# Gate and up projections with 480 moving columns: one pass of the high weights over high and low tokens

## The chip, the cores and the metric

The kernel runs on one core of one Trainium2 chip. The time is device time in microseconds (us) of the whole program, from several executions. A core has five engines with instruction streams of their own: TensorE (PE in the profile, with its weight loads as PEld), VectorE (DVE), ScalarE (ACT), GpSimd (POOL) and SyncE (SP), which issues most DMAs here. They meet through semaphores.

## The reference

One layer on x of 8 batches x 64 tokens x 1024:

```python
x = x + cross_attention(layernorm(x), context)   # 8 x 1601 context rows and the 64 new ones
x = x + self_attention(layernorm(x))             # 16 heads, rotary, causal
xn = layernorm(x)
weights = golden_weights(xn, Wr, temperature)    # which of 8 experts, with which weight
gate = jnp.einsum('btd,edf->betf', xn, Wg)
up = jnp.einsum('btd,edf->betf', xn, Wu)
h = jax.nn.silu(gate) * up
e_out = jnp.einsum('betf,efd->betd', h, Wd)
x = x + jnp.einsum('bte,betd->btd', weights, e_out)
```

All is float32. The cross attention uses one head of width 1024. Each expert has three 1024 x 1024 matrices.

## The kernel before, in words

**Two parts for a float32.** Every float32 operand of a product is split into a high part (rounded to fp32r) and a low part (the rest). A product is made of three matmuls: high x high, high x low, low x high (`three`, L1425 to L1428; which of its three lines carries which pair depends on the argument order). Weights and context stream in as *units* of 128 x 2048 float32 (1 MB). SP loads a unit into a ring slot `raw` (L426), ScalarE copies it to `hi` (L628), VectorE subtracts to get `lo` (L939), and then TensorE uses it. `hi` and `lo` have four slots (RING). ScalarE and VectorE split unit k + 3 (AHEAD) in the program's order before their own work for unit k.

**Experts.** For each expert the tokens that chose it, 240 at most (CAP), are gathered, turned (L1903) and split: `xg[:, c, 0:240]` holds the high parts of feature chunk c, `xg[:, c, 240:480]` the low parts, side by side. An expert has 12 units. Units 0 to 7 (f in the code) each hold 128 gate rows and 128 up rows (j = 0, 1), 8 chunks c each. So one unit is 2 x 8 x 3 = 48 matmuls of 240 columns into one PSUM bank `ps[:, f % 2, ...]`, gate in its first half and up in its second. Then ScalarE makes silu of the gate out of PSUM (L904), VectorE multiplies by up out of PSUM (L1390), rounds to `h_hi` (L1393) and subtracts to `h_lo` (L1395). `h_split` counts these. Units 8 to 11 are the down projection, 96 matmuls of 512 columns into banks `Y_BANK`; ScalarE scales them into y (L912), and GpSimd adds y to the output by an indirect DMA (L531).

**What binds the order.** TensorE may begin unit f (from 2 on) only when `h_split` says that unit f - 2, whose bank it takes over, is done. After unit 2 TensorE multiplies the next expert's token list (`list_item`, L1891), for which VectorE builds `sel` and `item_list` after its work for unit 1 (`build_list`, L1346, L1348). VectorE begins each expert with `take_target` (L1364, L1366), which waits until all scatters of the expert before have landed. ScalarE begins it with the split of unit 3, which waits for unit 0 (`gu_ready`). Units are written out in the program's text; experts 0 to 6 are a loop, and the last one follows it.

**Cross attention.** Batches b = 0 to 7 follow each other; while the values of batch b are used, the keys of b + 1 are multiplied. `ATTENTION` is the list of units, and each engine's `attention` goes through it. For the first batch, ScalarE takes the exponentials of the scores (`exps`, L692) in its step for the last key unit (u = 6); TensorE needs them for `turn_weights(0)` (L1551), which stands before unit 3 of the next batch's keys.

## Time and profile before

| | us |
|---|---|
| median of 3 runs | 1269.14 |
| the runs | 1261.70, 1269.14, 1269.29 |
| the profiled execution, its own time | 1264.38 |
| its span | 1262.6 |
| TensorE busy | 1200.4 (95%) |
| VectorE busy | 818.9 (65%) |
| ScalarE busy | 633.1 (50%) |

The profile is of one execution. Its time exceeds the span by 1.8 us. The cross attention ends near 425 us, the self attention and the router follow, and the experts run from 709 us to the end. Busy shares are over the whole span; a TensorE matmul counts as busy from its start to the modelled end of its pipeline, so matmuls overlap in these numbers, and the pace is read from start to start.

### The profile page before, as it was taken

The numbers are of one execution on the slowest core, as the hardware profiler recorded it, in microseconds if no ns is written. First come the engines' busy times: TensorE is split into PE (matmuls) and PEld (weight loads), VectorE is DVE, ScalarE is ACT, GpSimd is POOL, SyncE is SP. The second block draws the span as 40 slices with busy tenths as digits, with TensorE's granted clock in tenths as the row PEclk, the third lists the DMA queues.
The fourth block names the chain that finished last, engine by engine and source line by source line (L and its number), as shares of the span: only waits on it lengthen the run. The fifth ranks groups of instructions, "written<-read, shape, count | busy, mean of one in ns | idle before, by whom it ended". The sixth has DMA issues, their size and how long they took to land.

```text
span 1262.6 us, 19328 instructions
## 1 busy us (share of the span) xinstructions
PE 1200.4 (95%) x7810; PEld 1050.4 (83%) x7810; DVE 818.9 (65%) x1026; ACT 633.1 (50%) x604; POOL 95.7 (8%) x74
## 2 busy tenths in 40 slices
PE   5999999999998999999997699999999999999996
PEld 5888777777777878888886698989898999999895
DVE  7336789989999566463565674747565655656465
ACT  4124889888897423123543345344444444454431
POOL 0010000000000000000000012121111111121202
PEclk9999899999999999999999799999999999999998
DMA  7445899999998624220234376766667666676642
GB/s 290 146 159 192 308 352 360 376 373 363 379 383 333 248 77 171 96 100 34 101 143 167 113 251 166 262 197 226 202 216 212 200 227 200 217 210 230 172 160 33
DMA packets 46872, 272.98 MB, mean 216 GB/s; under 512 B 5880, under 2 KB 6024, under 8 KB 18528
## 3 DMA queue, kind: packets, MB, share of 16 engines
q1 hardware_dynamic: 36768, 243.48, 52.8%
q0 software_dynamic: 10048, 28.71, 9.4%
q8 instruction: 40, 0.66, 0.2%
q14 instruction: 16, 0.13, 0.0%
HBM read 255.92 MB, written 16.25 MB: 216 GB/s over the span
## 4 chain that ended last, share of the span: by engine, by line
PE 77%; DVE 8%; ACT 6%; issue 4%; DMA 4%; POOLq 0%; SPq 0%; POOL 0%; ACTq 0%; DVEq 0%
PE ps L1426 21%; PE ps L1427 21%; PE ps L1428 21%; PE ps L1539 6%; DVE lo L939 5%; ACT hi L628 4%; DMA out<-y,target 3%; PE ps L1652 2%; PE ps L1903 1%; PE ps L1587 1%; DVE stats L943 1%; ACT scores L692 1%; DMA raw<-weights 1%; PE ps L1745 1%; PE ps L1729 1%
## 5 line engine op out<-in xcount | busy, mean ns | idle before, releaser
L939 DVE TENSOR_TENSOR lo<-raw,hi 128x2048 fp32r<-128x2048 f32 (+1 forms) x198 | 443.4, 2251 | 160.3 <-ACT hi L628 157.9
L628 ACT ACTIVATE hi<-raw 128x2048 fp32r<-128x2048 f32 (+1 forms) x198 | 370.5, 1882 | 252.2 <-PE ps L1428 241.3
L1426 PE MATMUL ps<-act_hi,hi 128*128 128x240 f32 (+2 forms) x1232 | 360.7, 293 | 7.4 <-DVE act_lo L965 4.1
L1428 PE MATMUL ps<-act_hi,lo 128*128 128x240 f32 (+2 forms) x1232 | 361.6, 294 | 0.0
L1427 PE MATMUL ps<-act_hi,hi 128*128 128x240 f32 x1024 | 282.8, 276 | 0.0
L1426 PEld LDWEIGHTS ps<-act_hi,hi 128*128 128x128 f32 x1232 | 234.2, 190 | 16.7 <-issue 5.4
L1428 PEld LDWEIGHTS ps<-act_hi,lo 128*128 128x128 f32 x1232 | 234.6, 190 | 6.9
L1427 PEld LDWEIGHTS ps<-act_hi,hi 128*128 128x128 f32 x1024 | 193.5, 189 | 0.3
L1426 PE MATMUL ps<-hi,act_hi 128*128 128x512 f32 x320 | 126.4, 395 | 0.0
L1428 PE MATMUL ps<-hi,act_lo 128*128 128x512 f32 x320 | 124.9, 390 | 0.0
L1427 PE MATMUL ps<-lo,act_hi 128*128 128x512 f32 x320 | 124.8, 390 | 0.0
L904 ACT ACTIVATE xq<-ps 128x240 f32<-128x240 f32 x64 | 23.7, 370 | 164.4 <-PE ps L1428 164.3
L1539 PE MATMUL ps<-hi,qs 128*128 128x512 f32 (+1 forms) x256 | 94.6, 381 | 7.8 <-DVE lo L939 7.8
L1426 PE MATMUL ps<-hi,h_hi 128*128 128x512 f32 x256 | 101.3, 396 | 0.0
L1427 PE MATMUL ps<-lo,h_hi 128*128 128x512 f32 x256 | 101.0, 394 | 0.0
L1428 PE MATMUL ps<-hi,h_lo 128*128 128x512 f32 x256 | 101.0, 394 | 0.0
L1652 PE MATMUL ps<-hi,pt 128*128 128x512 f32 (+1 forms) x208 | 86.4, 415 | 6.4 <-DVE lo L939 5.1
L1539 PE MATMUL ps<-lo,qs 128*128 128x512 f32 (+1 forms) x256 | 91.5, 372 | 0.0
L1652 PE MATMUL ps<-lo,pt 128*128 128x512 f32 (+1 forms) x208 | 83.2, 400 | 0.0
L939 DVE TENSOR_TENSOR lo<-raw_more,hi 128x2048 fp32r<-128x2048 f32 (+2 forms) x38 | 76.8, 2032 | 8.3 <-ACT hi L628 8.3
L1427 PE MATMUL ps<-act_lo,hi 128*128 128x512 f32 (+1 forms) x208 | 78.4, 377 | 0.0
L531 POOL DMA_INDIRECT out<-y,target x32 | 51.8, 1617 | 307.3 <-ACT y L912 305.1
(228 smaller groups left out, 1431.2 us busy)
## 6 DMA issues: line engine op xcount, KB each, us to landing
raw<-weights SPq DMA_DIRECT2D x124, 1024.0 KB, 4.9
raw<-keys SPq DMA_DIRECT2D x36, 1024.0 KB, 5.8
raw<-context SPq DMA_DIRECT2D x31, 1024.0 KB, 8.3
raw_more<-context SPq DMA_DIRECT2D x17, 1024.0 KB
raw_more<-keys SPq DMA_DIRECT2D x12, 1024.0 KB
xq<-x_in SPq DMA_DIRECT2D x4, 512.0 KB, 6.8
raw_more<-weights SPq DMA_DIRECT2D x4, 512.0 KB
new_keys_t<-kvs POOLq DMA_DIRECT2D x8, 256.0 KB, 3.6
```

The lines of the kernel that those rows point to most:

```text
L531: pool.indirect_dma_start(out_d.rearrange("t (g d) -> (t g) d", g=2), bass.IndirectOffsetOnAxis(ap=target[0:R, g, n:n + 1], axis=0), y[0:R ...
L628: act.activation(part(hi, k, kind), part(raw, k, kind), ACT.Copy).then_inc(hi_done, 1)
L692: act.activation(S[rows, :], S[rows, :], ACT.Exp, bias=nb[rows, :], scale=SCALE, accum_out=sums[rows, :]).then_inc(p_ready, 1)
L904: act.activation(silu[:, k % 2, :], ps[:, k % 2, 0:CAP], ACT.Silu).then_inc(silu_done, 1)
L939: dve.tensor_tensor(part(lo, k, kind), part(raw, k, kind), part(hi, k, kind), ALU.subtract).then_inc(lo_done, 1)
L943: steps.done(dve.bn_stats(stats[:, t, h, :], x[:, t, h * HALF:(h + 1) * HALF]))
L1426: pe.matmul(out, a_hi, b_hi, start=first, stop=False)
L1427: pe.matmul(out, a_hi, b_lo, start=False, stop=False)
L1428: return pe.matmul(out, a_lo, b_hi, start=False, stop=last)
L1539: ins = pe.matmul(scores_at(j, slice(0, P)), qs[:, s % 2, cc, :], buf[:, k % RING, c * w:(c + 1) * w], start=(cc == 0 and b == 0), stop=(c ...
L1587: ins = pe.matmul(out, O[:, c * P:(c + 1) * P], twice[:, 0:QL], start=True, stop=(s < LATE))
L1652: ins = pe.matmul(ps[:, 6 + h, :], pt[rows, kc, :], buf[rows, k % RING, at], start=(kc == 0 and b == 0), stop=(kc == NCH - 2 and b == 1))
```

## The change

Three edits. First, the gate and up products: the matmul of the high weights now has 480 moving columns, high and low tokens in one pass, and a second matmul of the low weights adds 240 columns. Gate and up of a unit take a bank each (`GU_BANK`: banks 0 and 1, or 6 and 7), and bank columns 240 to 480 hold a partial sum that has to be added: ScalarE copies these out of PSUM for gate and up (480 columns in all), VectorE adds the first halves out of PSUM to the copy in SBUF (`gate_up`), ScalarE makes silu of the gate, and VectorE multiplies, both out of SBUF. The first down half uses banks 0 and 1 and waits for `h_split` of unit 6 (7) in its first unit and of unit 7 (8) in its second. TensorE waits at an expert's end until the first two y are copied. Second, `gate_up` lies over x, so ScalarE waits once for the copy of x to the output; bank 7 held the first list, so unit 0 waits for `first_listed`. Third, the exponentials of batch 0 move behind the split of one more unit.

```diff
--- before.py
+++ after.py
@@ -308,6 +308,9 @@
         rows_turned = sem("rows_turned")
         xg_hi = sem("xg_hi")
         xg_done = sem("xg_done")
+        first_listed = sem("first_listed")
+        gu_copied = sem("gu_copied")
+        gu_added = sem("gu_added")
         gu_ready = sem("gu_ready")
         h_split = sem("h_split")
         h_padded = sem("h_padded")
@@ -383,7 +386,7 @@
             earlier_expert = route_c[:, CAP + NE:CAP + NE + NE * NE]
             token_id, token_p, token_t = (route_c[:, CAP + NE + NE * NE + j * TT:CAP + NE + NE * NE + (j + 1) * TT]
                                           for j in range(3))
-        silu = xq[:, TT * D:TT * D + 2 * CAP].rearrange("p (s n) -> p s n", s=2)
+        gate_up = xq[:, 0:4 * CAP].rearrange("p (s j n) -> p s j n", s=2, j=2)
         spare = xq[:, TT * D:TT * D + 2 * TT * NE * NE].rearrange("p (s n) -> p s n", s=2)
         logits_t = xq[0:NE, TT * D:TT * D + TOK]
         xg = act_hi
@@ -552,7 +555,8 @@
         LIST_BANK = 5
         SUM_AT = (NCH - 8) * QL + 8
         FIRST_BANK = 7
-        Y_BANK = (6, 2)
+        Y_BANK = (0, 2)
+        GU_BANK = (0, 6)
         LN_BANK = 4
         LOGITS_BANK = 3
         LOGITS_T_BANK = 2
@@ -754,6 +758,8 @@
                         block_copy(ATTENTION[n - 1][2])
                     if what == "keys":
                         s = b - 1
+                        if u == 0 and s == 0:
+                            exps(0)
                         if u == 0 and copied < blocks_before(n):
                             new_v_copy(copied)
                             copied += 1
@@ -768,7 +774,6 @@
                             if b == 0:
                                 new_v_copy(copied)
                                 copied += 1
-                                exps(0)
                     elif what == "values":
                         s = b
                         if u == 0 and s == B - 1:
@@ -900,8 +905,14 @@
 
                         split(u0 + k + AHEAD, PER_EXPERT, e, used=(gu_ready, 8 * e + 1) if k == 0 else None)
                     if k < 8:
+                        bank = GU_BANK[k % 2]
                         act.wait_ge(gu_ready, 8 * e + (k + 1))
-                        act.activation(silu[:, k % 2, :], ps[:, k % 2, 0:CAP], ACT.Silu).then_inc(silu_done, 1)
+                        if k >= 2:
+                            act.wait_ge(h_split, 8 * e + (k - 1))
+                        act.activation(gate_up[:, k % 2, :, :], ps[:, bank:bank + 2, CAP:2 * CAP],
+                                       ACT.Copy).then_inc(gu_copied, 1)
+                        act.wait_ge(gu_added, 8 * e + (k + 1))
+                        act.activation(gate_up[:, k % 2, 0, :], gate_up[:, k % 2, 0, :], ACT.Silu).then_inc(silu_done, 1)
                     if k == 7 and more:
                         turned_hi(e + 1)
                     if k in (9, 11):
@@ -913,6 +924,7 @@
                                            scale=target_w[0:R, n:n + 1]).then_inc(y_done, 1)
 
             turned_hi(0)
+            act.wait_ge(scattered, 16)
             with act.Fori(0, NE - 1) as e:
                 item(e, U_FFN, False, True)
             item(NE - 1, U_FFN, False, False)
@@ -1292,8 +1304,9 @@
             dve.tensor_copy(item_list[:, :, :], token_w[:, :, 0:1, :].rearrange("p t a k -> p t (a k)"))\
                .then_inc(sel_built, 1)
             dve.wait_ge(list_summed, 1)
-            dep(dve.tensor_copy(listed[0:R, :, 2:LIST], ps[0:R, FIRST_BANK, 0:NT * 8].rearrange("p (n k) -> p n k", k=8)
-                                [:, :, 2:LIST]))
+            dve.tensor_copy(listed[0:R, :, 2:LIST], ps[0:R, FIRST_BANK, 0:NT * 8].rearrange("p (n k) -> p n k", k=8)
+                            [:, :, 2:LIST]).then_inc(first_listed, 1)
+            dve.wait_ge(first_listed, 1)
 
             def slot_values():
                 steps.done(dve.tensor_tensor(slot_token[0:R, :], listed[0:R, :, 0], listed[0:R, :, 1], ALU.add))
@@ -1386,13 +1399,16 @@
                     if more or k + AHEAD < PER_EXPERT:
                         split(u0 + k + AHEAD, PER_EXPERT, e)
                     if k < 8:
+                        bank, both = GU_BANK[k % 2], gate_up[:, k % 2, :, :]
+                        gate, up = both[:, 0, :], both[:, 1, :]
+                        dve.wait_ge(gu_copied, 8 * e + (k + 1))
+                        dve.tensor_tensor(both, ps[:, bank:bank + 2, 0:CAP], both, ALU.add).then_inc(gu_added, 1)
                         dve.wait_ge(silu_done, 8 * e + (k + 1))
-                        steps.done(dve.tensor_tensor(silu[:, k % 2, :], ps[:, k % 2, CAP:2 * CAP],
-                                                     silu[:, k % 2, :], ALU.mult))
+                        steps.done(dve.tensor_tensor(gate, up, gate, ALU.mult))
                         steps.wait()
-                        steps.done(dve.tensor_copy(h_hi[:, k, 0:CAP], silu[:, k % 2, :]))
+                        steps.done(dve.tensor_copy(h_hi[:, k, 0:CAP], gate))
                         steps.wait()
-                        dve.tensor_tensor(h_lo[:, k, 0:CAP], silu[:, k % 2, :], h_hi[:, k, 0:CAP],
+                        dve.tensor_tensor(h_lo[:, k, 0:CAP], gate, h_hi[:, k, 0:CAP],
                                           ALU.subtract).then_inc(h_split, 1)
                     if k == 1 and more:
                         build_list(e + 1, bass.ds(e + 1, 1))
@@ -1920,13 +1936,18 @@
                         pe.wait_ge(h_split, 8 * e + (f - 1))
                     elif f == 0:
                         pe.wait_ge(routed, 1)
+                        pe.wait_ge(first_listed, 1)
                     for j in range(2):
                         for c in range(C):
                             if f == 0 and j == 0 and c % 2 == 0:
                                 pe.wait_ge(xg_done, 4 * e + (c // 2 + 1))
                             at = slice(j * D + c * P, j * D + (c + 1) * P)
-                            ins = three(ps[:, f % 2, j * CAP:(j + 1) * CAP], hi[:, k % RING, at], lo[:, k % RING, at],
-                                        xg[:, c, 0:CAP], xg[:, c, CAP:2 * CAP], c == 0, c == C - 1)
+                            out = ps[:, GU_BANK[f % 2] + j, 0:2 * CAP]
+                            if c == C - 1:
+                                pe.matmul(out[:, 0:CAP], lo[:, k % RING, at], xg[:, c, 0:CAP], start=False, stop=False)
+                            ins = pe.matmul(out, hi[:, k % RING, at], xg[:, c, 0:2 * CAP], start=c == 0, stop=c == C - 1)
+                            if c < C - 1:
+                                pe.matmul(out[:, 0:CAP], lo[:, k % RING, at], xg[:, c, 0:CAP], start=False, stop=False)
                     ins.then_inc(gu_ready, 1)
                     if f == 2 and more:
                         list_item(e + 1)
@@ -1938,7 +1959,7 @@
                         k = u0 + 8 + 2 * g + half
                         if g == 0:
 
-                            pe.wait_ge(h_split, 8 * e + 4 * (half + 1))
+                            pe.wait_ge(h_split, 8 * e + (7 + half))
                         elif half == 0 and more:
                             pe.wait_ge(xg_done, 4 * e + 8)
                         if half == 0:
@@ -1955,6 +1976,8 @@
                                 ins.then_inc(y_ready, 1)
                         if half == 0:
                             ins.then_inc(unit_used, 1)
+                if more:
+                    pe.wait_ge(y_done, 4 * e + 3)
 
             pe.wait_ge(sel_built, TT)
             first_list(LIST_BANK, slice(0, 2), token_w[:, :, 0, :]).then_inc(index_summed, 1)
```

ScalarE, in the last expert (no loop counters between its rows), units 0 to 2; L628 splits a unit, L904 is silu. Before:

```order
L628 ACTIVATE hi<-raw 128x2048 [waits gu_ready,landed3]
L904 ACTIVATE xq<-ps 128x240 [waits gu_ready]
L628 ACTIVATE hi<-raw 128x2048 [waits gu_ready,landed0]
L904 ACTIVATE xq<-ps 128x240 [waits gu_ready]
L628 ACTIVATE hi<-raw 128x2048 [waits gu_ready,landed1]
L904 ACTIVATE xq<-ps 128x240 [waits gu_ready]
```

Now, with the split at L632, the copy at L912 and silu at L915:

```order
L632 ACTIVATE hi<-raw 128x2048 [waits gu_ready,landed3]
L912 ACTIVATE xq<-ps 128x480 [waits gu_ready]
L915 ACTIVATE xq<-xq 128x240 [waits gu_added]
L632 ACTIVATE hi<-raw 128x2048 [waits gu_ready,landed0]
L912 ACTIVATE xq<-ps 128x480 [waits gu_ready]
L915 ACTIVATE xq<-xq 128x240 [waits gu_added]
L632 ACTIVATE hi<-raw 128x2048 [waits gu_ready,landed1]
L912 ACTIVATE xq<-ps 128x480 [waits h_split,gu_ready]
```

Each silu now stands behind a copy and a wait for VectorE (`gu_added`), and ahead of the next split.

VectorE in the same place; L939 subtracts for `lo`, L1390 multiplies. Before:

```order
L939 TENSOR_TENSOR lo<-raw,hi 128x2048 [waits hi_done]
L1390 TENSOR_TENSOR xq<-ps,xq 128x240 [waits silu_done]
L1393 CAST h_hi<-xq 128x240 [waits dve_step]
L1395 TENSOR_TENSOR h_lo<-xq,h_hi 128x240 [waits dve_step]
L939 TENSOR_TENSOR lo<-raw,hi 128x2048 [waits hi_done]
L1390 TENSOR_TENSOR xq<-ps,xq 128x240 [waits silu_done]
```

Now, with the subtraction at L951, the new addition at L1405 and the multiplication at L1407:

```order
L951 TENSOR_TENSOR lo<-raw,hi 128x2048 [waits hi_done]
L1405 TENSOR_TENSOR xq<-ps,xq 128x480 [waits gu_copied]
L1407 TENSOR_TENSOR xq<-xq 128x240 [waits silu_done]
L1409 CAST h_hi<-xq 128x240 [waits dve_step]
L1411 TENSOR_TENSOR h_lo<-xq,h_hi 128x240 [waits dve_step]
L951 TENSOR_TENSOR lo<-raw,hi 128x2048 [waits hi_done]
L1405 TENSOR_TENSOR xq<-ps,xq 128x480 [waits gu_copied]
```

An addition of 480 columns has come between the subtraction for `lo` and the multiplication, and the latter waits for the silu that comes after the addition.

ScalarE at the first batch's exponentials (`scores,cols`), from the last score copy. Before:

```order
L686 ACTIVATE scores<-ps 64x130 [waits s_evac,s_ready]
L745 ACTIVATE new_v<-ps 128x4x128 [waits block_turned]
L692 ACT_TABLE_LOAD
L692 ACTIVATE scores,cols<-scores,cols 64x1665 [waits negmax_ready]
L628 ACTIVATE hi<-raw_more 128x2048 [waits s_ready,landed5]
L628 ACTIVATE hi<-raw 128x2048 [waits unit_used,landed0]
```

Now:

```order
L690 ACTIVATE scores<-ps 64x130 [waits s_evac,s_ready]
L749 ACTIVATE new_v<-ps 128x4x128 [waits block_turned]
L632 ACTIVATE hi<-raw_more 128x2048 [waits s_ready,landed5]
L696 ACT_TABLE_LOAD
L696 ACTIVATE scores,cols<-scores,cols 64x1665 [waits negmax_ready]
L632 ACTIVATE hi<-raw 128x2048 [waits unit_used,landed0]
```

The split of one unit (`raw_more`) has moved ahead of the table load and the exponentials; the next unit's still follows them.

## Rows read from the trace of the kernel before

Lines of groups: line, engine, operation, out<-in, shapes, count | busy us, mean ns of one | idle us before them and what ended it. Lines of a timeline: start us, duration us, engine, line, operation, out<-in, shapes, count [idle us before <- what ended it]. Lines of stretches: from:to, length, then busy us (instructions) of PE, PEld, DVE, ACT and POOL, granted TensorE clock, DMA share, GB/s.

**Rows 1.** The page: the span, and the granted TensorE clock in 40 slices.

```profile
span 1262.6 us, 19328 instructions
...
PEclk9999899999999999999999799999999999999998
```

**Rows 2.** Groups of instructions by line and form, expert stage, 709 us to the end.

```profile
L1426 PE MATMUL ps<-act_hi,hi 128*128 128x240 f32 x1024 | 281.9, 275 | 3.2 <-DVE h_lo L1395 3.1
...
L1372 DVE TENSOR_TENSOR act_hi<-ps,act_hi 128x480 fp32r<-128x480 f32 x31 | 18.4, 649 | 0.4
...
L887 ACT ACTIVATE act_hi<-ps 128x480 fp32r<-128x480 f32 x30 | 14.9, 577 | 0.7 <-PE ps L1903 0.5
```

**Rows 3.** Timeline of ScalarE, from expert 0's last outputs to expert 1's unit 5.

```profile
774.98 0.69 ACT L912 ACTIVATE y<-ps,target_w 120x512 f32<-120x512 f32 x1 [0.87 <-PE ps L1428]
777.77 0.69 ACT L912 ACTIVATE y<-ps,target_w 120x512 f32<-120x512 f32 x1 [2.10 <-PE ps L1428]
...
783.16 1.92 ACT L628 ACTIVATE hi<-raw 128x2048 fp32r<-128x2048 f32 x1 [3.40 <-PE ps L1428]
785.09 1.28 ACT L904 ACT_TABLE_LOAD   x1
786.38 0.37 ACT L904 ACTIVATE xq<-ps 128x240 f32<-128x240 f32 x1
...
805.55 0.37 ACT L904 ACTIVATE xq<-ps 128x240 f32<-128x240 f32 x1 [3.21 <-PE ps L1428]
...
810.94 0.37 ACT L904 ACTIVATE xq<-ps 128x240 f32<-128x240 f32 x1 [3.21 <-PE ps L1428]
```

**Rows 4.** Timeline of VectorE in expert 1, units 0 and 1.

```profile
784.76 0.24 DVE L1364 TENSOR_SCALAR target<-slot_token 120x2 int32<-120x2 f32 x2 [8.32 <-DMA out<-y,target]
...
785.15 2.29 DVE L939 TENSOR_TENSOR lo<-raw,hi 128x2048 fp32r<-128x2048 f32 x1
787.36 0.40 DVE L1390 TENSOR_TENSOR xq<-ps,xq 128x240 f32<-128x240 f32 x1
...
788.11 0.41 DVE L1395 TENSOR_TENSOR h_lo<-xq,h_hi 128x240 fp32r<-128x240 f32 x1
...
791.56 0.41 DVE L1395 TENSOR_TENSOR h_lo<-xq,h_hi 128x240 fp32r<-128x240 f32 x1
...
792.90 0.17 DVE L1348 COPY item_list<-token_w 128x20 bf16 x1
```

**Rows 5.** Timeline of TensorE: units 2 and 3 of expert 1 begin, the list between.

```profile
788.58 0.38 PE L1426 MATMUL ps<-act_hi,hi 128*128 128x240 f32 x1
...
794.08 0.56 PE L1891 MATMUL ps<-item_list,sel 128*120 128x5 bf16 x8
794.49 0.36 PE L1426 MATMUL ps<-act_hi,hi 128*128 128x240 f32 x1
```

**Rows 6.** Timeline of TensorE: router logits, stationary operand of 8 columns.

```profile
682.87 0.22 PE L1427 MATMUL ps<-act_lo,wr_hi 128*8 128x128 f32 x1
682.93 0.23 PE L1428 MATMUL ps<-act_hi,wr_lo 128*8 128x128 f32 x1
```

**Rows 7.** Timeline of ScalarE around the first batch's exponentials.

```profile
131.28 1.69 ACT L692 ACTIVATE scores<-scores,cols 64x1665 f32<-64x1665 f32 x1 [0.75 <-DVE cols L1009]
...
132.96 1.90 ACT L628 ACTIVATE hi<-raw_more 128x2048 fp32r<-128x2048 f32 x1
```

**Rows 8.** Timeline of TensorE in the same place.

```profile
133.20 0.40 PE L1551 MATMUL ps<-ident,scores 64*128 64x64 f32 x2 [0.27 <-ACT scores L692]
...
137.24 0.80 PE L1539 MATMUL ps<-hi,qs 128*128 128x512 f32 x1 [2.71 <-DVE lo L939]
...
143.84 0.40 PE L1426 MATMUL ps<-act_hi,hi 128*128 128x512 f32 x1
```

**Rows 9.** Busy time of the engines in two stretches, from the busy time by stretch.

```profile
138.00:143.00 5.00, 5.00 (x14) 3.90 (x13) 4.94 (x5) 4.72 (x7) 0.00 (x0) 0.50 0.98 357
...
1060.00:1062.00 2.00, 0.62 (x5) 0.43 (x5) 1.93 (x5) 2.00 (x3) 0.00 (x0) 1.00 0.13 16
```

## The prediction, made before the changed kernel ran

> **What bounds the kernel now.** I read the page first: TensorE is busy 95% of the span and its granted clock is near full nearly everywhere [rows 1]. The groups by form for the expert stage then show that the 240-column matmuls wait for almost nothing, 3.2 us in all, and what they wait for is `h_lo` [rows 2]. So in the expert stage the pace of TensorE is the time. That pace is read from start to start: ScalarE's silu of two neighbouring units, each released by TensorE, start 5.39 us apart (810.94 - 805.55), so a matmul of 240 columns takes 5.39 / 48 = 112 ns [rows 3]. The two y copies of one down half are 2.79 us and 12 matmuls apart, 232 ns for 512 columns [rows 3]. The timelines of VectorE and ScalarE at an expert's start show a second thing: the end of the chain that lets unit 2 begin. VectorE's `take_target` starts at 784.76 when the last scatter has landed, the subtraction for unit 3 at 785.15, the multiplication at 787.36, and `h_lo` ends at 788.52 [rows 4]; TensorE begins unit 2 at 788.58 [rows 5]. Unit 2 is thus already set by this chain and not by unit 1, with hardly a wait yet. Everything the change adds to VectorE and ScalarE between 787.36 and 788.52 moves unit 2.
>
> **Term 1, TensorE's pace.** Per chunk three matmuls of 240 columns (336 ns) become one of 480 and one of 240: as many columns, one weight load fewer. The trace has no 480. At 2.4 GHz 512 columns are 213 ns and were 232, so 19 ns were added; 240 are 100 and were 112, 12 added. A 480 is then 200 + 13 to 18, and a pair 325 to 330 ns, near the row of 512, which it is nearest to. Upper bound of the pair: 336, if a matmul costs in proportion to its columns. Lower bound: matmuls of 128 columns behind an 8-column weight load start every 60 ns, where 53 are the columns [rows 6], so nothing but 6 to 7 ns per matmul is left: 313. I take 327.5, a unit of 16 x 327.5 = 5.24 us, 0.14 less (0.11 to 0.17; by the bounds 0 to 0.38).
>
> Against this stands a rule of the Trainium skill (TensorE: Matmul & The Clock Gate, Back-to-back issue gap): a warm matmul follows the last after N / 2.4 + 2.5 ns. By that 240 columns would be 102.5 and 512 be 215.8; the trace has 112 and 232, so it does not agree. By the rule a pair would be 305 ns and a unit 4.88 us, my sum would end 15 us lower; the first rival goes that way.
>
> **Term 2, the start of each expert.** In the changed program VectorE's first step after the subtraction is the new addition of 480 columns out of PSUM. It starts where the multiplication started, 787.36, since ScalarE's copy (0.58 by the same form, [rows 2]) follows the split at 783.16, 1.92 long, and is over near 785.6 [rows 3]. The addition takes 0.65 [rows 2]. Only then silu: its table load (1.28) is over by then, silu takes 0.37 [rows 3], and two handovers about 0.03 each. The multiplication, now at 787.36 + 0.65 + 0.07 + 0.37 = 788.45, runs as long as before (`h_lo`, which reads SBUF for both inputs, takes 0.41 at the same size [rows 4]). So unit 2 begins 1.09 later, at 789.67. What units 0 and 1 gained is lost there, all of it.
>
> **Term 3, the list.** ScalarE's split of unit 4 now stands behind the silu that waits for the addition. From one `h_split` to the next the path is: split 1.91, subtraction 2.29, addition 0.65, silu 0.37, which with the turn to the multiplication is 5.10 us (handovers and overlaps of neighbours, 0.1 each, counted). Before it was 791.56 - 788.11 = 3.45 [rows 4]. Unit 1's `h_lo` then ends at 789.61 + 5.10 = 794.71, `build_list`, queued behind it on VectorE, takes until 1.10 later (791.97 to 793.07 before [rows 4]), 795.81, and TensorE, which comes from unit 2 at 789.67 + 5.24 = 794.91, waits 0.96 for it. The list takes 0.41, so unit 3 begins at 796.28 and not at 794.49 [rows 5]: 1.79 late. From here 5.10 is less than 5.24, `h_split` stays ahead, and units 3 to 7 give back 5 x 0.14 = 0.70. The new wait for unit 6 ahead of the down projection is met: turning the gathered rows stands between. Unit 7's has a half of 24 matmuls of 512, 5.6 us, before it.
>
> Per expert that is + 1.09. Expert 0 starts without a target wait, and unit 2 has 0.15 us to spare there (my reading of its rows; an estimate): + 0.94. The last builds no list: 1.09 - 6 x 0.14 = + 0.25. Experts: 6 x 1.09 + 0.94 + 0.25 = **+ 7.7 us** (+ 6.5 to + 9.2 for a unit 0.17 to 0.11 us shorter).
>
> **At nothing.** The waits for x's copy and for `first_listed`: VectorE itself waits for that copy at the start of expert 0 and for the list before it splits the first tokens, both ahead of unit 0. The wait for y at an expert's end: these copies are made while the second down half (two units, 11 us) runs. The longer use of VectorE in units 3 to 7, and SP's loads behind a later `lo`: covered as long as the 5.10 stays under the unit; uncovered each 0.1 us costs 4 us over the kernel. Overflow work after the last expert's units begins 2 to 3 us later relative to TensorE, under 11 us of down projection.
>
> **Term 4, the exponentials.** Before, ScalarE waits 0.75 us for the maximum, works from 131.28 to 132.96, and only then splits the unit of which TensorE is short: TensorE idles 2.71 us until 137.24, and then runs 16 matmuls until 143.84, 0.41 us each, mostly at half clock [rows 7 to 9]. Now that split comes at once, at about 129.2 to 131.1, the table load to 132.4, the exponentials to 134.1. TensorE waits for them until 134.3 (133.20 before), turns the weights in 1.3 (133.20 to 134.53, where the idle time begins), has the unit ready, does its 8 matmuls to 137.5, waits for the next `lo` (split at 134.1 to 136.0, subtraction to 138.3) and reaches the block unit at about 140.3, 3.5 us before 143.84. If the clock still falls, or later transfers are the bound anyway, down to 0 is left. ScalarE's next long wait in that stretch is for TensorE, so I take **- 3.0 us** (0 to - 3.6).
>
> **Sum.** + 7.7 - 3.0 = + 4.7 us. The profiled execution was 1264.38 (span 1262.6 and 1.8 around it), so 1269.1 on its terms; the median of the three runs is 4.8 higher, and the mean of all four is 1266.1. I go from the mean: 1266.1 + 4.7 = **1271 us**.
>
> **Rivals.**
> *The pair is cheap*, 313 ns as by the lower bound. Units of 5.01 us gain 0.38; 35 + 6 of them count (units 3 to 7 of seven experts, 2 to 7 of the last), 15.6, against the 13.5 lost by terms 2 and 3: - 2.1, with term 4 - 5.1: 1261. For it: one load fewer per chunk. Against: 512 columns show no such pace. Chance 0.15. (By the rule of the Trainium skill above, 305 ns, it would be 1256.)
> *The exponentials bring nothing*: 1266.1 + 7.7 = 1274. For it: the DMA share is 0.98 right behind the place [rows 9], so transfers could set the end of the stage. 0.15.
> *The clock falls at the new stalls.* TensorE will idle about 1.6 us ahead of unit 2 and 1 us ahead of the list. At 1060 it idled 1.38 of 2.0 us and the clock stayed 1.00; after 2.71 us at 134 to 137 it was 0.50 [rows 8, 9]. 16 matmuls took 6.6 us there, where 232 ns each would be 3.7: 2.9 us a fall. It decides from the gap ahead of unit 2: if 1.6 us are enough, eight falls, + 23: 1294, slower by 2%. If only the longest (expert 5, 1.38 + 1.09 + 0.28) falls, + 3, in my range. 0.08 for all.
> *VectorE and ScalarE keep less step than I sum*, a cycle of 5.5 and not 5.1, stalls in units 4 to 7: 4 x 7 x 0.26 = + 7: 1278. 0.07.
> My forecast keeps 0.55.
>
> **How the numbers follow.** Range 1256 to 1281: down to the cheap pair less the 5 us by which the fastest run of before lies under the mean, up to the slow cycle with one fall of the clock. About 1% (12.7 us) is what a measurement of this kernel tells from no change. Faster by more needs the cheapest pair and a gain in the exponentials together: 0.06. Slower by more: the clock, or the slow cycle on the high side: 0.14. The rest 0.80.
>
> **What would show it.** Right: start to start 213 to 218 ns after a 480, silu 5.2 to 5.3 us apart in units 3 to 7; unit 2 begins 0.06 after `h_lo` with over 1 us idle ahead of it, the list waits for `item_list` about 1 us; experts start 1.1 us longer apart; the block unit near 140.3, no half clock at 138. Wrong: silu 5.0 apart (cheap pair); no idle ahead of unit 2; a granted clock under 1 in the expert stage; an addition or a silu longer than 0.65 and 0.37; the cross attention's end not earlier.

## The result, and the profile after

The changed kernel took 1276.36 us (median of 7 runs, 1273.06 to 1280.95), the kernel before 1265.39 beside it (median of 7, 1261.64 to 1269.29). The ratio is 1.0099, 95% interval 1.0078 to 1.0119: slower by 1%, 11.0 us by the medians and 12.5 by the ratio. I had forecast + 4.7 us on a mean of 1266.1, so 1271 with a range of 1256 to 1281. The time lies in that range and the direction was right, but the step of + 4.7 us (0.4%) is less than half of the measured one, and the interval excludes it.

The profiled execution of the changed kernel took 1280.95 us. It is the slowest of the seven, and its span is 16.4 us longer than that of the profile before, more than the medians differ. So single events of this profile are weighed below with further profiles. Its page, and the groups of the expert stage that answer to [rows 1, 2]:

```profile
span 1279.0 us, 17463 instructions
...
PEclk9999999999999999999997999999999999999998
```

```profile
L1948 PE MATMUL ps<-act_hi,hi 128*128 128x480 f32 x1024 | 343.6, 391 | 18.4 <-DVE h_lo L1411 18.4
L1405 DVE TENSOR_TENSOR xq<-ps,xq 128x480 f32<-128x480 f32 x64 | 41.8, 653 | 2.3 <-ACT xq L912 1.0
L912 ACT ACTIVATE xq<-ps 128x480 f32<-128x480 f32 x64 | 36.2, 566 | 69.3 <-PE ps L1948 69.3
L915 ACT ACTIVATE xq<-xq 128x240 f32<-128x240 f32 x64 | 25.9, 404 | 90.5 <-DVE xq L1405 90.5
```

The gate and up matmuls waited 3.2 us for `h_lo` before [rows 2]; now it is 18.4. The addition took 0.653 us and the copy 0.566, as forecast (0.65 and 0.58); the silu took 0.404 where I had 0.37.

VectorE in expert 1, units 0 and 1, against [rows 4] (start, duration, idle and its cause in brackets):

```profile
781.89 0.24 DVE L1377 TENSOR_SCALAR target<-slot_token 120x2 int32<-120x2 f32 x2 [8.44 <-DMA out<-y,target]
...
782.28 2.29 DVE L951 TENSOR_TENSOR lo<-raw,hi 128x2048 fp32r<-128x2048 f32 x1
784.49 0.65 DVE L1405 TENSOR_TENSOR xq<-ps,xq 128x480 f32<-128x480 f32 x1
785.61 0.41 DVE L1407 TENSOR_TENSOR xq<-xq 128x240 f32<-128x240 f32 x1 [0.47 <-ACT xq L915]
...
786.37 0.41 DVE L1411 TENSOR_TENSOR h_lo<-xq,h_hi 128x240 fp32r<-128x240 f32 x1
...
791.50 0.41 DVE L1411 TENSOR_TENSOR h_lo<-xq,h_hi 128x240 fp32r<-128x240 f32 x1
```

From `take_target` to the end of `h_lo` it is 786.78 - 781.89 = 4.89 us, and it was 788.52 - 784.76 = 3.76: + 1.13, where I had 1.09. From one `h_lo` to the next it is 5.13; I had 5.10. The chain is as forecast. TensorE against [rows 5], units 2 and 3 of expert 1 with the list between:

```profile
784.96 0.38 PE L1948 MATMUL ps<-act_hi,hi 128*128 128x480 f32 x1
786.84 0.49 PE L1948 MATMUL ps<-act_hi,hi 128*128 128x480 f32 x1 [1.50 <-DVE h_lo L1411]
...
793.07 0.60 PE L1907 MATMUL ps<-item_list,sel 128*120 128x5 bf16 x8 [0.74 <-DVE item_list L1361]
793.53 0.46 PE L1948 MATMUL ps<-act_hi,hi 128*128 128x480 f32 x1
```

Unit 2 waits 1.50 us and the list 0.74. The profile counts idle time from the modelled end of the last matmul; from start to start the list comes 793.07 - 786.84 = 6.23 us behind unit 2, and I had 5.24 + 0.96 = 6.20. ScalarE's copies of units 3 to 5, each released by TensorE, give the pace, against [rows 3]:

```profile
799.13 0.57 ACT L912 ACTIVATE xq<-ps 128x480 f32<-128x480 f32 x1 [1.11 <-PE ps L1948]
...
804.45 0.57 ACT L912 ACTIVATE xq<-ps 128x480 f32<-128x480 f32 x1 [1.28 <-PE ps L1948]
...
809.76 0.57 ACT L912 ACTIVATE xq<-ps 128x480 f32<-128x480 f32 x1 [1.36 <-PE ps L1948]
```

A unit takes 5.32 us here, not 5.24. The matmuls themselves, in unit 2 of the same expert:

```profile
788.25 0.38 PE L1948 MATMUL ps<-act_hi,hi 128*128 128x480 f32 x1
788.47 0.27 PE L1950 MATMUL ps<-act_hi,lo 128*128 128x240 f32 x1
788.58 0.38 PE L1948 MATMUL ps<-act_hi,hi 128*128 128x480 f32 x1
```

A pair takes 0.33 us from start to start, 0.22 of it for the 480 columns. And in expert 5 the last scatter lands late; VectorE, TensorE, and two stretches with the granted clock and the DMA share as the third and second number from the end:

```profile
1063.03 0.24 DVE L1377 TENSOR_SCALAR target<-slot_token 120x2 int32<-120x2 f32 x2 [10.81 <-DMA out<-y,target]
```

```profile
1067.97 0.77 PE L1948 MATMUL ps<-act_hi,hi 128*128 128x480 f32 x1 [3.86 <-DVE h_lo L1411]
1068.54 0.40 PE L1950 MATMUL ps<-act_hi,lo 128*128 128x240 f32 x1
1068.74 0.61 PE L1948 MATMUL ps<-act_hi,hi 128*128 128x480 f32 x1
...
1069.35 0.61 PE L1948 MATMUL ps<-act_hi,hi 128*128 128x480 f32 x1
```

```profile
1060.00:1062.00 2.00, 2.00 (x15) 1.81 (x14) 0.00 (x0) 1.98 (x3) 0.00 (x0) 1.00 0.09 15
...
1066.00:1071.00 5.00, 3.03 (x10) 2.68 (x11) 3.84 (x6) 2.66 (x3) 0.00 (x0) 0.66 0.61 210
```

Unit 0 of this expert began at 1053.36, so the landing is 9.67 us behind it, where expert 1 had 7.31. For the last 3 us hardly a DMA engine works (0.09 of the sixteen at 1060 to 1062). So the transfer was not short of bandwidth; it has a tail, and no run shows what it is made of. TensorE idles 3.86 us, and then a pair 480 + 240 takes 0.61 us (1068.74 to 1069.35) instead of 0.33: half clock, until 1070.99. In four of eight experts, 4 to 7, the granted clock fell behind the gap ahead of unit 2 in this execution.

The cross attention, against [rows 7, 8] (ScalarE's exponentials, then TensorE's wait for them, the unit behind it and the block unit):

```profile
132.46 1.69 ACT L696 ACTIVATE scores<-scores,cols 64x1665 f32<-64x1665 f32 x1
```

```profile
134.38 0.40 PE L1567 MATMUL ps<-ident,scores 64*128 64x64 f32 x2 [1.34 <-ACT scores L696]
...
135.63 0.71 PE L1555 MATMUL ps<-hi,qs 128*128 128x512 f32 x1
...
141.02 0.39 PE L1442 MATMUL ps<-act_hi,hi 128*128 128x512 f32 x1
```

The block unit begins at 141.02 instead of 143.84, forecast 140.3; the idle time of 2.71 us is gone. The half clock isn't, which I had not forecast: the granted clock is 0.81 at 132 to 138 and 0.88 at 138 to 143, where the kernel before had 0.88 and 0.50. Expert 0 begins at 704.82 instead of 709.46. Of these 4.6 us, 1.5 are not the change's: one stretch near 409 us ran at full clock this time, and the lead over the profile before grew from 2.9 to 4.4 us there. Before, and then after:

```profile
405.00:415.00 10.00, 9.07 (x54) 7.79 (x54) 5.54 (x9) 4.19 (x6) 0.00 (x0) 0.83 0.72 290
```

```profile
405.00:415.00 10.00, 9.07 (x50) 7.58 (x49) 7.08 (x9) 6.12 (x7) 0.00 (x0) 1.00 0.54 199
```

### The profile page after: what moved, and what is told of

The parts are those of the page before. It is cut to its first block, busy times and chain, and to the rows that moved or that the text cites. A ratio compares the mean times of both kernels' runs of the same rounds, so it can differ in the third digit from the quotient of the medians.

```text
span 1279.0 us, 17463 instructions
## 1 busy us (share of the span) xinstructions
PE 1199.2 (94%) x6786; PEld 1015.0 (79%) x6786; DVE 859.6 (67%) x1090; ACT 669.0 (52%) x668; POOL 96.8 (8%) x74
## 4 chain that ended last, share of the span: by engine, by line
PE 74%; DVE 9%; ACT 6%; issue 5%; DMA 5%; POOLq 0%; SPq 0%; POOL 0%; DVEq 0%; ACTq 0%
PE ps L1442 13%; PE ps L1444 13%; PE ps L1443 13%; PE ps L1948 13%; PE ps L1555 7%; PE ps L1950 6%; DVE lo L951 4%; ACT hi L632 4%; DMA out<-y,target 4%; PE ps L1668 2%; PE ps L1919 1%; PE ps L1603 1%; PE ps L1947 1%; DVE stats L955 1%; ACT scores L696 1%
## 5 line engine op out<-in xcount | busy, mean ns | idle before, releaser
L951 DVE TENSOR_TENSOR lo<-raw,hi 128x2048 fp32r<-128x2048 f32 (+1 forms) x198 | 443.5, 2252 | 159.6 <-ACT hi L632 157.8
L632 ACT ACTIVATE hi<-raw 128x2048 fp32r<-128x2048 f32 (+1 forms) x198 | 369.9, 1879 | 241.3 <-PE ps L1444 206.3
L1948 PE MATMUL ps<-act_hi,hi 128*128 128x480 f32 x1024 | 343.6, 391 | 18.4 <-DVE h_lo L1411 18.4
L1950 PE MATMUL ps<-act_hi,lo 128*128 128x240 f32 x896 | 247.6, 276 | 0.0
L1948 PEld LDWEIGHTS ps<-act_hi,hi 128*128 128x128 f32 x1024 | 188.7, 192 | 45.7 <-DVE h_lo L1411 15.7
L1950 PEld LDWEIGHTS ps<-act_hi,lo 128*128 128x128 f32 x896 | 173.5, 194 | 3.7
L1442 PE MATMUL ps<-act_hi,hi 128*128 128x512 f32 (+1 forms) x208 | 78.5, 377 | 4.1 <-DVE act_lo L977 4.1
L951 DVE TENSOR_TENSOR lo<-raw_more,hi 128x2048 fp32r<-128x2048 f32 (+2 forms) x38 | 76.8, 2032 | 2.5 <-ACT hi L632 2.5
L1444 PE MATMUL ps<-act_hi,lo 128*128 128x512 f32 (+1 forms) x208 | 78.1, 376 | 0.0
L915 ACT ACTIVATE xq<-xq 128x240 f32<-128x240 f32 x64 | 25.9, 404 | 90.5 <-DVE xq L1405 90.5
```

What stands on the lines that cost most here:

```text
L632: act.activation(part(hi, k, kind), part(raw, k, kind), ACT.Copy).then_inc(hi_done, 1)
L915: act.activation(gate_up[:, k % 2, 0, :], gate_up[:, k % 2, 0, :], ACT.Silu).then_inc(silu_done, 1)
L951: dve.tensor_tensor(part(lo, k, kind), part(raw, k, kind), part(hi, k, kind), ALU.subtract).then_inc(lo_done, 1)
L1442: pe.matmul(out, a_hi, b_hi, start=first, stop=False)
L1444: return pe.matmul(out, a_lo, b_hi, start=False, stop=last)
L1948: ins = pe.matmul(out, hi[:, k % RING, at], xg[:, c, 0:2 * CAP], start=c == 0, stop=c == C - 1)
```

## The experiments

Twelve runs were made, ten of edited kernels and one more of each of the two, in three groups, each group on one chip beside the kernel before (medians 1263.34, 1263.69 and 1262.81 us). A ratio is always to the kernel before beside it, and across groups the ratios are compared. *Landing* is the start of `take_target` less the start of unit 0.

**One edit alone.** The kernel before with nothing but the exponentials moved:

```diff
+                        if u == 0 and s == 0:
+                            exps(0)
...
-                                exps(0)
```

> The kernel before with only the move of the first batch's exponentials. Theory A (TensorE leads this stretch, the unit it lacks is ready 3.6 us sooner and the half clock behind it goes): the first expert's unit 0 starts at 704.8 as in the changed kernel, not at 709.5, and the whole is 4.4 to 4.7 us shorter than before, about 1261. Rival (the gain of the changed kernel's cross attention was run-to-run scatter, or is taken back by transfers): within 1.5 us of before.

1261.47 us (12 runs, 1257.92 to 1267.19), ratio 0.9983 (0.9964 to 1.0001). Expert 0 began at 705.79, 3.7 us earlier in the profiled execution, while the medians differ by 1.9. A gain somewhere from 0 to 4.5 us, under the 4.4 to 4.7 that I expected by the medians; it speaks for term 4 and doesn't settle its size. The counterpart is the changed kernel with the exponentials put back:

> The changed kernel with the first batch's exponentials put back where the kernel before has them; everything in the experts is the change's. Theory (the exponentials' move was worth 2 to 4 us): unit 0 of expert 0 begins near 709 instead of 705, TensorE stands idle for over 2 us near 134 again, and the time is 2 to 4.5 us above the changed kernel's, ratio to the kernel before 1.012 to 1.013. Rival (the move brought nothing): ratio 1.010.

1277.07 us, ratio 1.0129 (1.0107 to 1.015). Against the changed kernel's first ratio that is 3 thousandths, 3.8 us; against the changed kernel on the same chip (1277.53, two runs) nothing. Its profile has the wait of over 2 us again, with the clock at 0.82 and not 0.50 in 138 to 143. The start of expert 0 (705.79) is a poor measure here, since these executions are already up to 1.5 us apart at 119 us. A better one is the time between two starts of VectorE's subtraction for `lo`, twelve such subtractions apart, near 119 and 149 us:

```
                          from      to     us
before                  119.53  151.54  32.01
before again            119.95  151.48  31.53
exponentials alone      119.35  147.99  28.64
changed                 119.64  148.70  29.06
changed again           120.28  148.89  28.61
changed, put back       118.80  149.49  30.69
```

So in the profiles the move is worth 2.5 to 3.4 us against the kernel before, and 1.6 to 2.1 against the run with the exponentials put back, in which the clock was at half for a shorter stretch. Term 4 had - 3.0. The medians allow less: 1.9 us in the first pair of kernels, and nothing to 3.8 in the second.

**The pair back to three passes** in 12 of 16 chunks per unit, with the banks, the addition and everything else of the change:

```diff
+                                if c < C - 1:
+                                    pe.matmul(out[:, 0:CAP], hi[...], xg[:, c, 0:CAP], ...)
+                                    pe.matmul(out[:, CAP:2 * CAP], hi[...], xg[:, c, CAP:2 * CAP], ...)
```

> The changed kernel where 12 of the 16 chunks of a unit are made by three passes of 240 columns into the same banks and not by 480 and 240 (chunks 0 and 7 of gate and up keep the pair). Theory A (a pair is worth 4 to 5 ns only, since a 480 takes 220): a unit of 5.38 to 5.40 us where 5.33 was, + 2 us over the kernel, 1278. Rival (the pair is worth 10 ns or more and something else slows the units): + 5 us or more.

1280.15 us, ratio 1.0129 (1.0096 to 1.0162). ScalarE's copies of units 3 to 5 in expert 1:

```profile
803.86 0.57 ACT L912 ACTIVATE xq<-ps 128x480 f32<-128x480 f32 x1 [1.95 <-PE ps L1956]
...
809.24 0.57 ACT L912 ACTIVATE xq<-ps 128x480 f32<-128x480 f32 x1 [1.87 <-PE ps L1956]
```

5.38 us a unit (5.373 by TensorE's own starts) against 5.315. The pair saves little: 0.06 us a unit for 12 of 16 chunks, 2.4 us over 41 units. The times say 3.8 us, by medians and ratios alike, but the two intervals overlap and this profile too has late landings.

**The landing out of the way.** VectorE takes `take_target` after its work for unit 2 and not at the expert's start, in the changed kernel and in the kernel before (the latter with the exponentials moved):

```diff
-                take_target(e)
...
+                    if k == 2:
+                        take_target(e)
```

> The changed kernel with take_target (the wait for the last scatter) moved from VectorE's start of an expert to behind its work for unit 2. Theory A (the chain addition, silu, multiplication behind the split sets unit 2; a late scatter only lengthens it, and the clock falls where the gap passes about 1.8 us): unit 2 begins 12.1 us after unit 0 in all experts, gaps of 1.5 us, no 3.9 and 4.8 us gaps, no half clock; 3 to 6 us less than the changed kernel, 1271 to 1273. Rival (the late landings are themselves the loss): back to about 1266.

> The kernel before with the exponentials moved and take_target behind unit 2, splits first as they were. Theory A (a late scatter costs the kernel before too, one for one beyond 0.2 us): unit 2 begins 10.9 us after unit 0 in all experts, 3 to 5 us less than with the exponentials alone (1261.5): 1257 to 1258, runs within 2 us of each other.

The changed kernel: 1268.48 us, ratio 1.0039 (1.0024 to 1.0054). The kernel before: 1256.9, ratio 0.9943 (0.992 to 0.9966). Every expert of the first is now alike, unit 2 12.0 us behind unit 0 and 69.2 us from expert to expert, with no stretch at half clock; of the second, 10.97 and 67.8. Its groups:

```profile
L1949 PE MATMUL ps<-act_hi,hi 128*128 128x480 f32 x1024 | 336.6, 385 | 10.0 <-DVE h_lo L1410 10.0
```

and those of the kernel before with the same edit:

```profile
L1428 PE MATMUL ps<-act_hi,hi 128*128 128x240 f32 x1024 | 281.4, 275 | 0.4 <-DVE h_lo L1395 0.2
```

Two things follow. Late landings and what comes of them cost the changed kernel 7.6 us (1.0099 to 1.0039) and the kernel before 5.1 by the ratios (0.9983 to 0.9943; 4.6 by the medians). And without them the edit of the experts costs 10.4 us by the two spans (1265.1 and 1254.7) and 0.0096 of 1263.5, 12.1 us, by the two ratios; I had summed 7.7. So most of what my sum missed is there before any landing is late.

**The order on ScalarE and VectorE.** In the changed kernel each unit's copy, addition, silu and multiplication stand ahead of the split of unit k + 3 and no longer behind it (and so do the lists and the turned tokens):

```diff
-                    if more or k + AHEAD < PER_EXPERT:
+                    if k >= 8 and (more or k + AHEAD < PER_EXPERT):
                         split(u0 + k + AHEAD, PER_EXPERT, e)
...
+                    if k < 8:
+                        split(u0 + k + AHEAD, PER_EXPERT, e)
```

> The changed kernel with ScalarE and VectorE doing the work of units 0 to 7 (copy, addition, silu, multiplication, h; lists and turned tokens too) ahead of the split of unit k + 3 and not behind it. Theory A (the loss is this order: the silu chain behind a split and the next split behind the chain): unit 2 begins 10.7 us after unit 0 unless a scatter lands late, no wait ahead of the list, 18 to 24 us less than the changed kernel, 1253 to 1258. Rival (the loss is the longer use of VectorE or a contention that the order does not change): less than 5 us of it.

1254.13 us, ratio 0.9928 (0.9905 to 0.995), 22 us under the changed kernel. TensorE's wait for `h_lo` is gone, and 1.4 us are left of the wait for the list:

```profile
L1951 PE MATMUL ps<-act_hi,hi 128*128 128x480 f32 x1024 | 335.5, 385 | 0.1
...
L1910 PE MATMUL ps<-item_list,sel 128*120 128x5 bf16 x56 | 4.2, 197 | 1.4 <-DVE item_list L1362 1.4
```

So what terms 2 and 3 name, the longer way of a unit's result behind a split, is the loss; with the other order the copy, the sum and the addition fit beside TensorE but for that wait. The next group, on another chip, shows what each part is worth once that order is there: the kernel before with the exponentials and this order, the changed kernel with this order and `take_target` late, and the kernel before with both.

> The kernel before (three passes of 240) with the exponentials moved and with the units' own work ahead of the split. Theory A: the kernel before lost only 0.3 us an expert at unit 2, so 2 us from the exponentials and 3 us here: 1258. Rival (the order, not its combination with the added copy and addition, is the loss): as fast as the changed kernel with that order, 1254.

> The changed kernel with the units' own work ahead of the split and take_target behind unit 2. Theory A: with the chain out of the way, late scatters reach unit 2 in few experts; 0 to 1 us less than with the order alone, 1253, and a scatter of the runs under 2 us.

> The same two moves and the exponentials' in the kernel before. What is left between this and the changed kernel with both is the pair of passes against three: Theory A (0.074 us a unit, 64 units): 4 to 5 us, so this at 1257 to 1258. Rival (the copy and the addition cost TensorE something besides the order): less than 3 us apart.

| order, take_target | three passes | pair |
|---|---|---|
| own work first | 1254.29 (0.9921) | 1254.13 (0.9928) |
| own work first, target late | 1255.36 (0.9928) | **1247.96** (0.9873, 0.9848 to 0.9899) |

The order helps the kernel before as well, 1254.29 us where I expected 1258. So of the 22 us, only the part by which the two kernels differed, 1.2% (1.0099 against 0.9983), was the edit's cost; the rest is the order's own gain. With the target early the pair gains nothing even then. With it late it gains 7.4 us, where I expected 4 to 5; I had also expected 1253 and not 1247.96 for the pair. That one is the fastest kernel of the study, 16 us under the kernel before. Against the kernel with the target early, its profile has no wait for the list (in experts 1 to 6 unit 3 begins 5.72 us behind unit 2 and not 6.10 to 6.24) and the shorter unit in six experts and not in two. Its units 3 to 5 in expert 1 are not at the pace of the changed kernel:

```profile
803.60 0.57 ACT L911 ACTIVATE xq<-ps 128x480 f32<-128x480 f32 x1 [1.70 <-PE ps L1952]
...
808.83 0.57 ACT L911 ACTIVATE xq<-ps 128x480 f32<-128x480 f32 x1 [1.72 <-PE ps L1952]
```

5.23 us a unit, the 5.24 that I had summed, with the same matmuls and no change to TensorE's program. Why the same pairs run at 5.23 in one place and 5.32 in another is open; the changed kernel itself has 5.23 in expert 2 and 5.32 in the others.

**The clock.** The changed kernel with TensorE kept at work ahead of unit 2, by 12 products of the identity that nobody reads:

```diff
+                    if f == 2:
+                        for _ in range(12):
+                            pe.matmul(ps[:, 4, 0:P], ident, ident, start=True, stop=True)
```

> The changed kernel with 12 more weight products on TensorE ahead of unit 2's first product in every expert: the identity against 128 of its own columns, into a bank that nothing reads at that time. They are extra work whose product nobody reads, about 12 x 0.109 = 1.3 us, laid into a gap in which TensorE stood idle for 1.2 to 4.8 us in the profile of the changed kernel. Theory (falls of TensorE's clock after this gap are a part of what the change cost): list wait to list wait stays at 6.7 in all experts instead of 7.15 to 7.39 in three, no stretch of units 2 and 3 runs at 0.50, and the time is 1.5 to 4 us under the changed kernel's, near 1273, ratio to the kernel before 1.007. Rival (the falls cost next to nothing, the late landings are all of it): the same ratio as the changed kernel, 1.010, or up to 1.011 where the products run beyond the gap.

1273.46 us (1270.34 to 1277.28), ratio 1.0087 (1.0067 to 1.0107). That is 1.5 us under the changed kernel's first ratio and 3.7 under its second (below), and the intervals overlap: the times don't show what the clock is worth. And the edit did more than I meant. The twelve products are 192 matmuls in the profile, 24 and not 12 in each expert:

```profile
L1937 PE MATMUL ps<-ident x192: 270/275/275, 714.8 to 1205.5; 128*128 128x128 f32 x192
```

They take 2.6 us and not 1.3, so unit 2 begins 13.2 us behind unit 0 where 12.0 to 12.3 is the undisturbed time of the changed kernel. The wait for the list shrinks by most of that, and unit 3 begins 18.96 us behind unit 0, against 18.7 in the changed kernel with the target late. So the run has a cost of its own, up to 0.3 us an expert, and its time can't price the falls. The profile shows that the clock stayed. Two landings were late here too, and after them:

```profile
1063.00:1071.00 8.00, 7.90 (x56) 7.23 (x54) 6.29 (x12) 4.46 (x5) 0.00 (x0) 1.00 0.52 166
...
1209.00:1217.00 8.00, 8.00 (x50) 7.31 (x49) 6.29 (x10) 4.23 (x5) 0.00 (x0) 1.00 0.52 157
```

The granted clock is 1.00 in both, against 0.66 at 1066 to 1071 in the changed kernel. From unit 0's `h_lo` to unit 7's takes 36.4 to 36.7 us in experts 0 to 6 and 36.0 in the last, as without a fall.

**Both kernels once more**, for a second profile each:

> The changed kernel once more, for a second profile. If the landing of an expert's last scatter varies by execution, it is late (over 8.4 us behind unit 0's start) in other experts than 5 and 7, TensorE's gap ahead of unit 2 is again longest there, and units 2 and 3 are at half clock in those experts whose gap is over 1.8 us. If it is a matter of place, the same two are late, by the same 2 to 3 us.

> The kernel before once more, for a second profile. If landings vary by execution, one or two of experts 1 to 7 are over 8.4 us behind unit 0's start, others than expert 5 perhaps; the gap ahead of unit 2 is over 1.8 us in fewer experts than in the changed kernel.

1277.53 us (two runs), ratio 1.0116 (1.0092 to 1.0141), and 1271.68 (one run, 6.1 us above the highest of the eleven of the kernel before beside it, so no measure of that kernel). Landings of experts 1 to 7, us behind unit 0's start:

```
                 1     2     3     4     5     6     7
before         7.19  7.31  7.28  7.59  8.50  7.11  7.99
before again   7.13  9.90  7.05  7.42  7.55  9.38  8.85
changed        7.31  7.15  7.63  7.67  9.67  7.87 10.60
changed again  8.57  9.36  6.82  7.36  7.39  7.47  8.50
```

Which expert is late changes with the execution, in both kernels, and not with the change. What happens then differs. The kernel before, expert 2 and expert 6 of its second profile (TensorE's idle time ahead of unit 2 was 2.78 and 2.26):

```profile
858.00:863.00 5.00, 4.21 (x23) 4.21 (x24) 4.88 (x11) 0.22 (x1) 0.00 (x0) 0.66 0.78 241
1134.00:1139.00 5.00, 4.53 (x40) 4.53 (x41) 4.92 (x11) 0.42 (x1) 0.00 (x0) 1.00 0.83 261
```

and the changed kernel's second profile, expert 1 (idle 2.75):

```profile
788.00:793.00 5.00, 4.92 (x16) 4.43 (x17) 3.83 (x6) 2.53 (x4) 0.00 (x0) 0.50 0.59 200
```

The time lost to falls, from the same span of units 0 to 7 less its undisturbed value, is 0, 3.2 and 1.7 us in three profiles of the old experts (before, before again, exponentials alone) and 3.7, 3.0 and 2.3 in three of the new (changed, changed again, exponentials back): 1.4 more in the mean. TensorE's idle time ahead of unit 2, less what it is in the kernels without landings there, is 2.9, 7.3 and 5.3 us over experts 1 to 7 in the old and 8.5, 6.2 and 4.1 in the new: 1.1 more in the mean. Both sums overlap between old and new, and three profiles a side are few. Together they agree with the 2.5 us of the four ratios (7.6 less 5.1).

## Why the prediction was wrong

**The step that failed is term 1, the pace: mis-sized by half.** I took 0.14 us a unit, 0.11 at the least, from an estimate near the row of 512 columns. Units 3 to 7 take 26.65 us and took 27.02, 0.074 each. Start to start a 480 is 221 ns and the 240 behind it 111, where 512 and 240 alone were 231 and 112: the 480 costs nearly its share of two 240s, which was my upper bound of the pair (336 ns; it is 332). With 41 units that count this is + 2.7 us, the largest part of what is missing, and with it the forecast would have been + 7.4. The value I summed exists, as the fastest kernel shows (5.23), but the changed kernel has it in few units. By the rule of the Trainium skill (TensorE: Matmul & The Clock Gate, Back-to-back issue gap), which the page gives for the isolated gap, a pair would be 305 ns; the trace has 327 to 332 and doesn't agree. The first rival, 313 ns, is out by the same rows. It was also priced too low: with a unit of 5.01 us the cycle of 5.10 from my own term 3 would have been the bound, so its 1261, and the 1256 below it, leave that out.

**The landing under the clock's rival: put at nothing.** I priced the gap ahead of unit 2 from one execution, in which the latest landing was expert 5's with 8.50 us, and gave falls 0.08 as a matter of all eight or of one. In the ten profiles that wait for the target at an expert's start, nine have one to three landings of 8.5 us or more, up to 10.6. Each moves unit 2 in both kernels; in the changed one it meets a TensorE that already idles over a microsecond there, and there gaps of 1.84 and more lost the clock. That is 2.5 us more than in the kernel before by the ratios, of which falls are 1.4 by few profiles. Gaps of 1.23 to 1.65 kept the clock in all experts seen, so the rival as I put it, all eight at 1.6 us, is out too. The truth lay between its two cases.

**Term 2, unit 2: right.** + 1.13 per expert in the chain, 1.09 forecast; + 1.03 from unit 0 to unit 2 in the two kernels with the target late. Expert 0 is like the others: it had no 0.15 us to spare.

**Term 3, the list: right.** From unit 2 to unit 3 it is 6.70 us instead of 5.91, + 0.79 where I had + 0.70.

**At nothing, the rest: right.** The undisturbed experts of the kernel with `take_target` late show no other wait, and the cycle of 5.13 stays under the unit: the fourth rival is out. The tail behind the last y copy is 9.3 against 8.8 us.

**Term 4: right in the profiles, open in the times.** The block unit came 2.8 us earlier, and the table of the first experiment has 2.5 to 3.4; the medians have 1.9. The second rival, nothing gained, is out by the profiles. That the clock would stay up at 138 was wrong.

In sum: 4.7 forecast + 2.7 (pace) + 0.3 (the rest of the undisturbed experts, 10.7 us from their starts where I had 7.7) + 2.5 (landings and clock) + 0 to 1 (exponentials) = 10.2 to 11.2, against 11.0 by the medians and 12.5 by the ratio. The undisturbed pair of kernels also differs by 1.7 us more in its ratios than in its spans; those 1 to 2 us stay open. The high end of term 1 to 3's sum should have read + 9.0 and not + 9.2 (41 units of 0.03 us); nothing else rests on it.

## What to carry to other kernels

Fewer or wider matmuls gain only what start to start times say, and the way of the result to the unit that waits for it is priced in the same sum: here 1.9 us more of way per expert outweighed 0.4 us of pace. Look at the order on the helping engines first. With each unit's own work ahead of the split of a later unit, both kernels stand 0.7 to 0.8% under the kernel before, and the edit costs nothing where it had cost 1.2%. With the wait on scatters out of that way too, the edit gains 0.6%. A wait that hangs on a DMA's landing has a distribution: read it over all repetitions, and in more than one execution, before a price is put on what follows it.

## What the runs showed of the hardware

- The same sequence of 480 and 240 columns has two paces in units 4 to 7 of the experts, 5.32 and 5.23 us for 16 pairs (221.5 + 110.7 and 217.7 + 109.0 ns start to start), with no wait and full granted clock in both. Three passes of 240 took 5.39 in all of them.
- Scatters of two times 120 rows landed 6.8 to 10.6 us behind the start of unit 0. Ahead of the landings at 8.8 us and later, the busy share of the DMA engines was 0.10 or less for the last 2 us.
- The size of TensorE's idle time alone doesn't tell whether the clock falls. In the experts 1.65 us and below kept it, 1.78 lost it in one profile, 1.81 and 1.83 kept it in two others that both lost it at 1.84, and 2.26 kept it once. A wait of 0.93 us between 405 and 410 us lost it in six of fourteen profiles and kept it in eight.
